# Macaron block on one core: bias products moved to the end of network 1, half the lowering of network 2 on VectorE, both networks' last two tiles in two pairs of banks, output bias added during the scores

## The reference

```
x = x + 0.5 * ffn(LN(x))          # network 1
x = x + attention(LN(x))          # 2048 x 2048 scores for each of the 2 batches
x = x + 0.5 * ffn(LN(x))          # network 2

ffn(x):       gate = q(x) @ q(w_gate).T;  up = q(x) @ q(w_up).T       # 704 each
              return q(silu(gate) * up) @ q(w_down).T
q(v):         blocks of 16 along the row, scale = max|block| / 6,
              each value rounded to the FP4 grid 0, .5, 1, 1.5, 2, 3, 4, 6, times scale
attention(x): Q, K, V = x @ W.T + b  (512 each);  softmax(Q K.T / 16) V @ Wo.T + bo
```

## Time and profile before

| | us |
|---|---|
| median of 3 runs | 1053.4 (1051.5 to 1054.3) |
| the profiled execution | 1055.0 |
| its span in the trace | 1053.1 |

### The profile page before, as it was taken

How to read it: one execution, slowest core, us unless ns; L and a number is a source line. 1 busy time by engine, 2 the same in 40 slices (tenths; PEclk the granted TensorE clock), 3 DMA queues, 4 the chain that set the end, 5 groups by cost and what they waited for, 6 DMA issues and landing times.

```text
span 1053.1 us, 16576 instructions
## 1 busy us (share of the span) xinstructions
PE 987.3 (94%) x5685; PEld 857.9 (81%) x5685; DVE 711.6 (68%) x1254; ACT 605.1 (57%) x1219; POOL 365.3 (35%) x551
## 2 busy tenths in 40 slices
PE   3899999999969899999999899999989999999995
PEld 2778888888868688888888788888877888988885
DVE  7678888888737455555568455555566778788772
ACT  5567777777744344554454344445445666666653
POOL 3346676767552000000014000000012555655643
PEclk9799999999979999999999999999998999999999
DMA  9000000000000000000000000000000000000000
GB/s 321 7 1 1 1 1 2 1 1 1 1 1 1 1 0 0 0 0 0 0 1 1 0 1 0 0 0 0 0 0 1 1 21 21 21 21 21 21 21 20
DMA packets 11528, 13.49 MB, mean 13 GB/s; under 512 B 849, under 2 KB 10577, under 8 KB 11473
## 3 DMA queue, kind: packets, MB, share of 16 engines
q1 hardware_dynamic: 11472, 12.79, 3.6%
HBM read 8.59 MB, written 4.19 MB: 12 GB/s over the span
## 4 chain that ended last, share of the span: by engine, by line
PE 82%; DVE 9%; ACT 3%; issue 3%; POOL 3%; DMA 0%; POOLq 0%; SPq 0%; DVEq 0%; ACTq 0%
PE bank L1271 21%; PE bank L1430 17%; PE bank L1456 11%; PE bank_b L1280 10%; PE bank L1172 6%; PE bank L1458 6%; PE bank L1176 5%; PE bank L1301 3%; POOL zq L438 2%; DVE probs L699 1%; PE bank L1407 1%; DVE grid L600 1%; DVE amax L572 1%; PE bank L1183 1%; DVE rounded L594 1%
## 5 line engine op out<-in xcount | busy, mean ns | idle before, releaser
L438 POOL TENSOR_TENSOR zq<-grid,s_neg 128x704 f32<-128x704 f32 (+2 forms) x192 | 179.5, 958 | 58.1 <-DVE grid L600 53.7
L1456 PE MATMUL bank<-v_hl,pT_hi 128*128 128x512 f32 x512 | 184.7, 402 | 0.0
L1111 ACT ACTIVATE pT_hi<-bank 128x512 fp32r<-128x512 f32 x127 | 75.6, 598 | 159.5 <-PE bank L1172 159.4
L1271 PE MATMUL bank<-w_hi,T_hi 128*128 128x512 f32 (+1 forms) x384 | 151.6, 395 | 3.0 <-ACT bqk L878 1.6
L355 POOL TENSOR_TENSOR var<-var,eps_all 128x1 f32<-128x1 f32 (+1 forms) x64 | 12.4, 194 | 407.8 <-ACT st_junk L919 407.8
L1271 PE MATMUL bank<-w_hi,T_lo 128*128 128x512 f32 (+1 forms) x384 | 145.9, 380 | 0.0
L1271 PE MATMUL bank<-w_lo,T_hi 128*128 128x512 f32 (+1 forms) x384 | 145.6, 379 | 0.0
L1458 PE MATMUL bank<-v_hl,pT_lo 128*128 128x256 f32 x512 | 143.9, 281 | 0.0
L759 DVE TENSOR_TENSOR pT_lo<-bank,pT_hi 128x512 fp32r<-128x512 f32 x127 | 87.5, 691 | 49.0 <-ACT pT_hi L1111 49.0
L1430 PE MATMUL bank<-k_hi,q_hi 128*128 128x512 f32 x256 | 109.7, 428 | 7.6 <-ACT probs L1106 7.6
L1456 PEld LDWEIGHTS bank<-v_hl,pT_hi 128*128 128x128 f32 x512 | 96.3, 188 | 21.6
(11 more groups left out here) (176 smaller groups left out, 2033.5 us busy)
## 6 DMA issues: line engine op xcount, KB each, us to landing
out<-x SPq DMA_DIRECT2D x7, 512.0 KB, 2.9
x<-in_L_attn_hidden_states SPq DMA_DIRECT2D x3, 1024.0 KB, 13.9
x<-in_L_attn_hidden_states SPq DMA_DIRECT2D x2, 512.0 KB, 7.1
wraw<-in_L_ffn_w_down SPq DMA_DIRECT2D x1, 704.0 KB, 8.5
wraw<-in_L_ffn_w_gate SPq DMA_DIRECT2D x1, 640.0 KB, 4.5
wraw<-in_L_ffn_w_up SPq DMA_DIRECT2D x1, 640.0 KB, 5.8
wq_s<-in_L_attn_Wq SPq DMA_DIRECT2D x1, 512.0 KB, 8.1
wk_s<-in_L_attn_Wk SPq DMA_DIRECT2D x1, 512.0 KB, 9.0
```

The costliest lines, as they stand in the source:

```text
L438: last = nc.gpsimd.tensor_tensor(out=blocks(zq[:, to:to + hi - lo]), in0=blocks(grid[:, lo:hi]), in1=spread(s_neg[:, par, lo // BLOCK:hi / ...
L1111: nc.scalar.activation(pT_hi[:, 4 * ch:4 * ch + 4, :].rearrange("p a q -> p (a q)"), transposed(b, i, ch), ACT.Copy).then_inc(phi_done, 1)
L1271: last = nc.tensor.matmul(gu[:, lo:hi], lhsT=T[:, par, HK + kd, :], rhs=w[:, kd, lo:hi], start=n == 0, stop=n == len(terms) - 1)
L1456: nc.tensor.matmul(bank_a[:], lhsT=pT_hi[:, t, :], rhs=v_hl[:, t, :], start=t == 0, stop=False)
```

## The change

**Start.** TensorE no longer makes the query bias and the bias rows there. The value-output product is split around the subtraction of round -2, its subtraction moves to round -1. On ScalarE `x_means(1)` moves behind the absolute value of chain tile -3, `normalise(3)` ahead of `x_variances(1)`. The key bias row is now made in round 29 of network 1 ahead of `chain_lower`, the value bias row behind the transposes of tile 31, the query bias behind the first key transposes.

**Rounds of network 1.** VectorE's `input_statistics` goes ahead of `product`. GpSimd's single `inverse_std` is replaced by `output_std` for four tiles in every fourth round.

**Rounds of network 2.** TensorE subtracts only in the second bank, ScalarE copies only that bank's low part; the first bank's low part is made by a new VectorE entry between the grid and the scaled y.

**Tails of both networks.** The transposes of tile 30 go to the two idle gate banks, those of tile 31 to `bank2` right behind. VectorE subtracts both tiles itself, multiplies the grid of tile 31 back itself (instead of GpSimd), and adds the last projection from PSUM to x. In network 1 it also normalises and multiplies the first group of keys ahead of that last residual.

**Keys, values, scores.** ScalarE measures tiles 30 and 31 in group 2 instead of ahead of the first key copy. GpSimd's four bias additions of a batch wait until all its values have their low part.

```diff
@@ banks
-        m_bank, bq_sum = bank4[:, 2, :], bank4[:, 2, 0:1 + KD]
+        m_bank = bank4[:, 2, :]
-        rk_sum, bv_sum = bank2[:, 0, 0:D], bank2[:, 0, D:2 * D]
+        rk_sum, bv_sum = bank4[:, 2, 0:D], bank4[:, 2, D:2 * D]
+        bq_sum = bank_a[:, 0:1 + KD]
+        def T_bank(k):
+            return bank5[:, 0:2, :] if k == NT - 2 else bank2[:]
@@ GpSimd
+            def output_std(g):
+                q = slice(4 * g, 4 * g + 4)
+                pool.wait_ge(stats_done, 4 * (g + 1))
...
-                    if hidden(c - 1):
+                    if hidden(c - 1) and c < NT:
                         residual(c - 1, 1 - par)
-                    if chain(c + 1):
+                    if chain(c + 1) and c + 1 < NT - 1:
                         quantised(c + 1, 1 - par)
-                    if f == 0 and hidden(c - 2):
-                        inverse_std(c - 2, c - 2)
+                    if f == 0 and c % 4 == 1 and c >= 5:
+                        output_std((c - 5) // 4)
...
                 def add_biases(g):
-                    pool.wait_ge(kn_done, b * NG + (g + 1))
+                    pool.wait_ge(vlo_done, (b + 1) * NG)
@@ VectorE
                         to_grid(c + 1)
+                    if f and hidden(c) and not late(c):
+                        lower_first(c, par)
                     if chain(c + 2):
                         scaled(c + 2)
...
+                def lower_first(k, par):
+                    dve.wait_ge(hi_done, number(f, k))
+                    nc.vector.tensor_tensor(out=T_lo[:, par, 0:4, :],
+                                            in0=bank2[:, 0, :].rearrange("p (n t) -> p n t", t=P),
+                                            in1=T_hi[:, par, 0:4, :].bitcast(F32),
+                                            op=ALU.subtract).then_inc(first_lo, 1)
...
                     blocks_of(c, par)
+                    if f == 0:
+                        input_statistics(c)
                     if hidden(c + 3):
                         product(c + 3)
-                    if f == 0:
-                        input_statistics(c)
+                    if c == NT - 2:
+                        quantised_last(1 - par)
+                        lower_late(c, par)
+                    if c == NT - 1:
+                        lower_late(c, par)
+                        if f == 0:
+                            normalise(0, 0)
+                            bias_products(0, 0)
+                        residual_last()
@@ ScalarE
+                    if late(c) and chain(c):
+                        chain_upper(c, par)
-                    if hidden(c - 1):
+                    if hidden(c - 1) and c < NT:
                         down_out(c - 1, 1 - par)
...
-                    t = slice(0, HK + KD) if hidden(k) else slice(HK, HK + KD)
+                    t = slice(4 if f else 0, HK + KD) if hidden(k) else slice(HK, HK + KD)
...
+                    if extra and c == NT - 1:
+                        bias_rows()
...
+                    if b == 0 and g == 2:
+                        statistics(NT - 2, NT - 2)
+                        statistics(NT - 1, NT - 1)
@@ TensorE
-                    for bank in range(2):
+                    for bank in range(1 if f else 0, 2):
...
+                    if extra and c == NT - 3:
+                        pe.wait_ge(gu_read, NT)
+                        key_bias_row()
+                    chain_lower(f, c, par)
...
+                def last_two():
+                    pe.wait_ge(gu_read, NT * (f + 1))
+                    transpose_chain(f, NT - 2)
+                    transpose_chain(f, NT - 1)
+                    if f == 0:
+                        value_bias_row()
+                    pe.wait_ge(late_lo, 2 * f + 1)
+                    pe.wait_ge(down_done, (NT - 1) * f + NT - 2)
+                    project_down(0)
+                    pe.wait_ge(late_lo, 2 * f + 2)
+                    pe.wait_ge(down_done, (NT - 1) * f + NT - 1)
+                    project_down(1)
+                    if f == 0:
+                        transpose_keys(0, 0)
+                        query_bias()
...
-            query_bias()
```

More of the change, by code:

```diff
@@ L234, in number, with number_lo, late @@
             return NCH * f + k + LEAD + 1
+        def number_lo(f, k):
+            return (NCH - 2) * f + k + LEAD + 1
+        def late(k):
+            return k >= NT - 2
+        def T_bank(k):
+            return bank5[:, 0:2, :] if k == NT - 2 else bank2[:]
         def early(k):
@@ L983, in step @@
                 def step(c, par):
-                    measured = f == 0 and hidden(c - 2)
+                    measured = f == 0 and 0 <= c - 2 < NT - 2
                     extra = f == 0
@@ L996, in step @@
                         upper_group(G1 + 2)
-                    if chain(c):
+                    if chain(c) and not late(c):
                         chain_upper(c, par)
-                    if extra and c == -2:
-                        nv_upper()
                     if extra and c == -1:
@@ L1006, in step @@
                         minus_mean(c - 2, c - 2)
-                    if chain(c):
+                    if chain(c) and not late(c):
                         chain_rest(c, par)
                     if extra and c == -2:
-                        bias_rows()
-                        nv_lower()
+                        nv_upper()
                     if extra and c == -1:
@@ L1217, in transpose_wo, with value_output_product @@
                 last.then_inc(aw["woT"], 1)
-            def value_output_product():
-                pe.wait_ge(aw["woT_s"], 2)
-                pe.wait_ge(wv_in, 16)
-                for dt in range(KD):
-                    last = product(nv_bank[:, dt * D:(dt + 1) * D], wv_s[:, :, dt * P:(dt + 1) * P], woT, dt == 0)
-                last.then_inc(aw["nv"], 1)
+            def value_output_product(dt):
+                if dt == 0:
+                    pe.wait_ge(aw["woT_s"], 2)
+                    pe.wait_ge(wv_in, 16)
+                product(nv_bank[:, dt * D:(dt + 1) * D], wv_s[:, :, dt * P:(dt + 1) * P], woT,
+                        dt == 0).then_inc(aw["nv"], 1)
             def value_output_lower():
@@ L1231, in value_output_lower, with key_bias_row, value_bias_row @@
                                  start=False, stop=True, skip_group_check=True).then_inc(aw["nv_sub"], 1)
[L1233 to L1236 removed]
+            def key_bias_row():
+                pe.wait_ge(aw["bcast"], 1)
+                product(rk_sum, bkB, wq_s).then_inc(aw["rows"], 1)
+            def value_bias_row():
+                product(bv_sum, bvB, woT, False).then_inc(aw["rows"], 1)
             def weight_lower(n):
@@ L1313, in step @@
                     extra = f == 0
-                    pe.wait_ge(lo_done, number(f, c) - 1 if c < NT else number(f, NT - 1))
+                    pe.wait_ge(lo_done, number_lo(f, c) - 1)
+                    if f and hidden(c - 1):
+                        pe.wait_ge(first_lo, c)
+                    if extra and c == -1:
+                        value_output_lower()
                     if gated and c < 0:
@@ L1414, in _ @@
                         pe.wait_ge(qT_done, k - 1)
-                    elif b:
+                    elif b == 0:
+                        pe.wait_ge(aw["bq_s"], 2)
+                    else:
                         pe.wait_ge(of_done, b * NS)
```

205 lines of the change are left out of this document (119 added, 86 removed).

## The result

The changed kernel takes 1028.35 us (median of 4 runs, 1027.9 to 1029.85); the kernel before, run beside it, 1052.66 us (1051.5 to 1054.3). The ratio is 0.9771 (95% interval 0.9751 to 0.9791): 24 us faster. The prediction said 1028.3. The profiled execution took 1027.9 us, its span is 1026.1.

The account below looks back on a forecast made before the run. TensorE was taken to bound most of the kernel, with waits at the joints and a second, equally long loop in network 2. Terms summed to -25.1 us, from the median 1053.4 to 1028.3; range 1020 to 1037.

Parts of the forecast that it names:

- The start: Up to the first hidden transposes: query bias and bias rows leave, -7.5 us (least -5, most -9).
- Network 1's rounds: 29 rounds of network 1: grouped deviations and statistics ahead of the product give -3 us (0 to -6).
- The tail: Network 1's tail, tile 29's transposes to first value product: earlier key eviction and value product, -6.8 us (-5 to -7.5).
- rival (c): Start bound by VectorE's weight work and half clock, tails by half clock: 7 to 9 us less gain, 1035 to 1037; chance 0.15.
- Keys and values: Both batches: bias products no longer held by GpSimd's additions, 6.5 us per group; -2.3 us in batch 1, -2.6 in batch 2.
- The additions during the scores: First score tile: GpSimd's fourth addition holds VectorE's small entries, first exponential 2.2 us later per batch; +4.4 us (0 to +4.8).
- rival (b): First score tile's small entries not held, or network 2's GpSimd multiply not lengthened: 1022 to 1024 us; chance 0.3.
- the +4.4: Forecast cost in us, over both batches, of the first score tile's small VectorE entries being held by the fourth addition.
- Network 2's rounds: One lowering matmul goes, but the two-round loop through GpSimd's multiply limits rounds to 7.23 us: -1.8 us (0 to -4).
- The end: After network 2's last rounds, from tile 29's transposes: last residual at +15.1 instead of +21.6; -5.5 us (-4 to -6.5).
- Rival (a): Network 2: GpSimd keeps the port pair across pieces, y waits: total 1056.2, chance 0.07; smaller form, one piece more, 1050, 0.05.
- 1.2 us of slack: Network 2's last four rounds: the loop through GpSimd's multiply was said to have this spare time, so they gain 0.9 us.

Follow-up runs that it names:

- one pair of banks: Changed kernel with tile 30 of both tails transposed into the usual banks and tile 31's transposes waiting for tile 30's low part: 1031.11 us, ratio 0.9776.
- y first: Changed kernel with VectorE making y ahead of the new subtraction in network 2, the down projection waiting later for that subtraction: 1025.2 us, ratio 0.9736.
- everything together: Changed kernel with y first, additions behind tile 1's queries, network 1's subtraction halved in rounds without statistics, and unread matmuls filling gaps: 1016.24 us, ratio 0.9682.
- the filled gaps: Changed kernel plus unread TensorE matmuls, 12 behind each batch's first score tile and 4 behind the query bias: 1023.49 us, ratio 0.9732.

## Why the prediction was right, and where its steps were not

**The start: right.** Transposes 0 came at 58.51 (about 58.5 had been said), the first SiLU at 38.40 (38.1). But 1.0 of the 7.7 us is only moved: round 0 takes 8.55 instead of 7.58, since TensorE waits there 0.77 us for ScalarE's copy of the last weight group. That wait ends at 60.37 instead of 67.05: 6.7 us is what the start gained for the rounds behind it.

**Network 1's rounds: the sum right, two sizes off.** The 28 rounds after the first gained 3.95, round 0 lost 0.97. What stays is what had been named, statistics that meet GpSimd's multiply, but in two rounds of four and not in one (7.80 and 7.38 us in the first group):

```profile
87.89 0.62 DVE L543 TENSOR_SCALAR nmean<-mv 128x4 f32<-128x4 f32 x1
```

It takes 0.62 us instead of 0.17, in each of the groups. The 28 rounds lose 3.0 us against 7.27 each, 0.5 to 0.6 per group of four, where I had kept 0.8. That the order carries all of it was shown by putting the statistics back.

**The tail: mechanism right, 0.5 us off.** The key eviction started 18.6 us after transposes 29 (+18 to +19 had been said), the first value product 21.1 (+20.6). The clock was at 1.00, so the half clock of rival (c) didn't come there.

**Keys and values: half right.** "Without it VectorE needs 5.1 us per group and TensorE 6.5" held in batch 2. For batch 1 "I take -2.3" missed by 1.0: the granted clock fell to 0.50 behind the first values for 3 us. At full clock the stretch is 25.1 to 25.2, so even -2.9 was there. The cause, the move of the additions, was wrong for batch 1, where they don't collide in the new order anyway.

**The additions during the scores: wrong step.** "Held by the fourth addition it comes 2.2 us later, in each batch" failed: the nearest row, an entry with one input and four elements, was taken for one with one input and one element. The negated bias wasn't held at all, the query entry was, and that costs at most 0.25 us a batch. So the mechanism of rival (b) is what happened, while its time, 1022 to 1024, didn't come. The scores did lose 1.5 us, for other reasons. Between the first two exponentials batch 1 lost 0.83, with the clock at 0.50 for 6.8 us instead of 3.4; that isn't the additions' doing, since two kernels that keep them where the change put them (one pair of banks, half of the subtraction in both networks) have 3.4 us and 13.3 there. Batch 2 lost 0.22 with the same 3.4 us at 0.50: the held query entry. The other score tiles, 12.97 us each instead of 12.95, added 0.7, and the joint to network 2 gave 0.35 back. The Trainium skill (VectorE: DVE Perf Modes, Mode 2×_2P) asks for an outermost dimension, other than one, that is even, or odd and equal in source and destination, before an operation with one tensor uses both ports; a one-element entry has no such dimension, a four-element entry has. The rows agree: 0.15 us for 128x1 beside an addition, 0.62 for 128x4 beside a multiply. Read with the sentence quoted in the prediction, that rule would have dropped the +4.4.

**Network 2's rounds: right loop, its size off.** "y waits for it to 924.95, and the 704-column piece waits for y" is what the rows show; the multiply grew by 0.08 and not by 0.17, the pair is 14.38 and not 14.47, and the rounds gained 2.7 and not 1.8: 2.0 in the first 25 (0.9 had been said) and 0.75 in the last four (0.9).

**The end: the missed interaction.** "-5.5" failed, because the walk of the last rounds left out whom y meets there. (Its own terms, 21.6 less 15.1, the residual's 0.4 and the clock's 0.4, add up to -5.7.) Rival (a), GpSimd keeping the pair from piece to piece, happened in no round: y gets in at the first boundary every time. But in the last three rounds the first piece is the 704 columns, and the boundary comes 0.8 us later. In two of them the "1.2 us of slack" covers that. In round 29 y ends 5.8 us after the transposes instead of the 4.4 of the kernel without the new subtraction, 0.6 of it the subtraction ahead of it and 0.8 the longer wait, and the end is 1.6 us longer. That kernel (17.4) and the one with y first (17.1) show it.

**How the sum came out.** Against the profiles it was 1.9 short: 2.9 too much cost for the additions and 0.9 too little gain in network 2's rounds, against 1.0, 0.8 and 0.5 too much gain for batch 1, the end and the tail. That the total still came out within 0.1 is luck: the profiled execution of before lay 1.6 above the median from which I counted and that of after 0.45 below its own, together what the sum was short of.

Left open: why the clock at the first values of batch 1 stayed up with the additions group by group, with half of the subtraction in both networks, and with everything together, and fell in the ten other profiles of changed kernels (the filled gaps alone among them); in the first of these three no instruction differs just ahead of that stretch. The score tiles of some kernels also take 12.97 us and of others 12.95, 0.7 us in all, which no row explains.

## What to carry to other kernels

When an entry is moved beside another engine's work, list every entry behind it in its stream and ask of each whether it uses the shared port: operand count, PSUM or not, one element or many. Then walk the first and the last rounds of a loop by themselves, since pieces that are missing there change who gets in first; here the order of two VectorE entries was worth 1.9 us at the end and 1.2 in 29 rounds. And price idle time of TensorE with what its clock does afterwards: a gap of 3.6 to 4.0 us in the first score tile cost another 1.6 to 2.8 us, and matmuls that nobody reads won it back.

## What the runs showed of the hardware

- The granted TensorE clock fell to 0.50 (1.2 GHz) for 3.4 or 6.8 us late in or behind an idle stretch of 3.6 to 4.0 us, not always for the same length in two executions of one kernel (first exponentials 14.11 and 14.52 us apart in batch 1, 13.52 and 14.25 in batch 2), and once not at all. With the idle time filled it stayed at 1.00 in four of four batches.
- A VectorE entry with two SBUF inputs that starts 0.16 us ahead of GpSimd's multiply takes 0.88 us, and 1.70 when it starts 0.44 us behind it, in a piece of 1.39 us. It gets in at the boundary of two GpSimd pieces (0.94 behind a first piece of 0.63 us), and the next piece waits for it (64 columns: 0.94 instead of 0.29). One with an operand in PSUM takes the same 0.68 or 0.69 ahead of the multiply or beside it.
- A VectorE entry with one input and one element took 0.15 us in the middle of a GpSimd addition, unheld; one with four elements took 0.62 instead of 0.17 beside a GpSimd multiply.
